# The ninth expert's first 1024 tokens in seven block products, and the next layers' units packed beside 24 steps instead of 40

## What is computed

```python
# L1: eight experts and one shared network, every token through all nine
g = jnp.einsum('bsd,edf->ebsf', h, Wg); u = jnp.einsum('bsd,edf->ebsf', h, Wu)   # D=256, F=1024
expert_outs = jnp.einsum('ebsf,efd->ebsd', jax.nn.silu(g) * u, Wd)
shared = jnp.einsum('bsf,fd->bsd', jax.nn.silu(h @ Sg) * (h @ Su), Sd)
x = x + (1.0 - sg) * jnp.einsum('be,ebsd->bsd', gating_probs, expert_outs) + sg * shared
# L2: adapter chosen per batch, residual, layer norm
h = jax.nn.relu(jnp.einsum('bsh,bha->bsa', x, w1) + b1)                          # A=64
y = x + jnp.einsum('bsa,bah->bsh', h, w2) + b2
x = x + layernorm(y) * gamma + beta
# L3: one 256x256 matrix chosen per batch
x = x + jnp.einsum('bnh,boh->bno', x, W) + b
```

## Time and profile before

| | us |
|---|---|
| median of 3 runs | 1586.52 (1586.15 to 1587.53) |
| the profiled execution, its own time | 1585.52 |
| its span, first to last instruction | 1583.7 |
| PE busy | 1574.8 (99%) |
| DVE, ACT, POOL busy | 1134.1, 931.1, 670.1 |

### The profile page before, as it was taken

The page is one execution under the profiler, slowest core; times in us unless marked ns, Lnnn a source line. Parts: engine busy times, 40 slices in busy tenths (PEclk is TensorE's granted clock), DMA queues, the critical chain, the costliest instruction groups (busy, mean ns, idle before and its releaser), DMA issues.

```text
span 1583.7 us, 22423 instructions
## 1 busy us (share of the span) xinstructions
PE 1574.8 (99%) x7916; PEld 1343.0 (85%) x7916; DVE 1134.1 (72%) x1685; ACT 931.1 (59%) x1683; POOL 670.1 (42%) x621
## 2 busy tenths in 40 slices
PE   9999999999999999999999999999999999999999
PEld 7888889999988888888888888888888888888898
DVE  6855556688789776776776776776776777657667
ACT  6655555565666666566656656666666665555444
POOL 7865544756777432442342342342342342028000
PEclk9999999999999999999999999999999999999999
DMA  4111105455421010010010010010010010022000
GB/s 161 55 53 53 54 27 188 159 174 173 162 92 40 14 41 27 14 41 27 14 40 27 14 41 27 14 40 28 14 41 28 14 40 27 14 58 78 14 14 28
DMA packets 31012, 85.98 MB, mean 54 GB/s; under 512 B 5030, under 2 KB 10534, under 8 KB 30774
## 3 DMA queue, kind: packets, MB, share of 16 engines
q1 hardware_dynamic: 30310, 83.21, 15.3%
q0 software_dynamic: 304, 1.10, 0.2%
q10 hardware_dynamic: 288, 0.26, 0.1%
HBM read 82.46 MB, written 2.10 MB: 53 GB/s over the span
## 4 chain that ended last, share of the span: by engine, by line
PE 94%; POOL 4%; issue 1%; DVE 1%; ACT 0%; DMA 0%; SPq 0%; POOLq 0%; ACTq 0%; DVEq 0%
PE up L674 13%; PE up L673 13%; PE up L672 13%; PE sum L441 12%; PE sum L443 12%; PE sum L442 12%; PE up L441 4%; PE up L442 3%; PE up L443 3%; PE up L449 2%; PE up L451 2%; PE up L450 2%; POOL expert_in L1479 1%; DMA raw<-in_shared 0%; POOL x_sums L1479 0%
## 5 line engine op out<-in xcount | busy, mean ns | idle before, releaser
L1291 ACT ACTIVATE hidden_hi<-up_tile 128x512 fp32r<-128x512 f32 x256 | 161.3, 630 | 188.5 <-DVE up_tile L2107 165.9
L2112 DVE TENSOR_TENSOR hidden_lo<-up_tile,hidden_hi 128x512 fp32r<-128x512 f32 x256 | 197.9, 793 | 44.7 <-ACT hidden_hi L1291 44.7
L2102 DVE TENSOR_TENSOR gate_tile<-up,gate_tile 128x512 f32<-128x512 f32 x192 | 130.1, 687 | 137.9 <-PE up L674 137.9
L441 PE MATMUL sum<-hidden_hi,down 128*128 128x512 f32 x512 | 199.3, 389 | 0.0
L672 PE MATMUL up<-x_sums,gate_up 128*128 128x512 f32 x512 | 199.2, 389 | 0.0
L443 PE MATMUL sum<-hidden_hi,down 128*128 128x512 f32 x512 | 199.2, 389 | 0.0
L673 PE MATMUL up<-x_sums,gate_up 128*128 128x512 f32 x512 | 199.2, 389 | 0.0
L442 PE MATMUL sum<-hidden_lo,down 128*128 128x512 f32 x512 | 199.2, 389 | 0.0
L674 PE MATMUL up<-x_sums,gate_up 128*128 128x512 f32 x512 | 199.2, 389 | 0.0
L2107 DVE TENSOR_TENSOR up_tile<-up_tile,gate_tile 128x512 f32<-128x512 f32 x192 | 183.5, 983 | 3.4 <-ACT gate_tile L1284 1.1
L1284 ACT ACTIVATE gate_tile<-gate_tile 128x512 f32<-128x512 f32 x192 | 119.7, 632 | 90.1 <-DVE gate_tile L2102 87.9
(11 more groups left out here) (332 smaller groups left out, 4014.6 us busy)
## 6 DMA issues: line engine op xcount, KB each, us to landing
raw<-in_experts SPq DMA_DIRECT2D x64, 512.0 KB, 3.2
raw<-in_l SPq DMA_DIRECT2D x51, 512.0 KB, 3.2
raw<-in_shared SPq DMA_DIRECT2D x23, 512.0 KB, 3.2
raw<-in_w SPq DMA_DIRECT2D x8, 256.0 KB, 2.5
x<-in_xT SPq DMA_DIRECT2D x3, 512.0 KB, 9.2
l_stage<-in_l SPq DMA_DIRECT2D x3, 512.0 KB, 4.1
out<-out_stage SPq DMA_DIRECT2D x6, 256.0 KB, 2.2
gate_w<-in_gw POOLq DMA_DIRECT2D x1, 1024.0 KB, 5.5
```

Of the source, the lines that this page charges most:

```text
L441: pe.matmul(out, wh, vh, start=start, stop=False)
L1291: A(hi[:, i], cu[:, i], ACT.Copy).then_inc(hi_done, 1)
L2102: V.tensor_tensor(t, ps, t, ALU.add).then_inc(c_done[m], 1)
L2112: V.tensor_tensor(lo[:, i], cu[:, i], hi[:, i].bitcast(f32), ALU.subtract).then_inc(lo_done, 1)
```

## The change

1. **Jobs.** The tokens 0 to 1023 of the ninth expert go as a seven-product block of their own: `PAIR_BLOCKS` has 17 entries, (8, 0) the last. `LAST_JOBS` keeps the jobs of 512, 256 and 256 tokens, 24 steps, whose weights are the blocks that the slots use (`gate_up`), with the one block that no slot needs in `plain_gate_up`.
2. **Units.** The five units stay (`UNITS`). Units 0 and 1 no longer follow a job each; their x is ready when the last slots are taken. `WHEN` places units 0 to 2 in steps 2 to 27 and unit 3 in 18 to 34; the last unit keeps its distance to the last step. Late weights are made at steps `LATE_AT` instead of one in each of steps 3 to 9.
3. **Places.** y, squares and the adapter's hidden tile get places of their own for unit 0, and two sets in `raw` for the others; the L3 matrices of batches 2 to 7 and the adapter matrices move to the weight sums' places; one pair of row sums instead of two. Some waits guard the new overlaps.
4. **Biases.** The L3 biases of batches 4 to 7 are loaded after the second adapter down product; `l2_up_stage(0)` waits for 12 bias loads: the eight of `b1` and four of L3.
5. **POOL's order.** The row sum and the power -1/2 of units 1 and 0 stand between late weights 5 and 7.

```diff
-LAST_JOBS = [(0, BLK), (BLK, BLK), (2 * BLK, BLK), (3 * BLK, S), (3 * BLK + S, S)]
+LAST_JOBS = [(2 * BLK, BLK), (3 * BLK, S), (3 * BLK + S, S)]
+UNITS = [(0, BLK), (BLK, BLK)] + LAST_JOBS
+LAST_STEPS = 8 * len(LAST_JOBS)
+ALL_STEPS = LAST_STEPS + 20
...
+PAIR_BLOCKS = [(e, j) for e in range(NS) for j in range(2)] + [(NS, 0)]
+NSS = len(PAIR_BLOCKS) * PAIRS
+LATE_AT = [1, 1, 3, 3, 4, 5, 6, 7]
...
-    (9, 10, 11, 11, 11, 11, 12, 12, 12, 13, 13, 13, 13, 14, 14, 14, 15, 15, 16, 16, 17, 18),
...
+    (2, 2, 4, 4, 4, 4, 5, 5, 5, 6, 6, 6, 6, 7, 7, 7, 8, 8, 10, 10, 11, 12),
+    (3, 6, 8, 9, 9, 9, 11, 11, 11, 12, 13, 12, 13, 15, 15, 15, 16, 16, 18, 18, 19, 19),
+    (10, 11, 13, 14, 14, 14, 17, 17, 17, 18, 19, 18, 19, 21, 21, 21, 22, 22, 24, 24, 26, 27),
+    (18, 18, 20, 21, 21, 21, 23, 23, 23, 24, 25, 25, 25, 26, 27, 27, 29, 29, 30, 32, 30, 34))]
...
-        def late_step(b):
-
-            return b + 3 if b < 6 else b + 2
...
         late_small = 2 * B
+        early_small = B + B // 2
...
                 sp.dma_start(b1[:, b:b + 1], b1_d[langs[b]]).then_inc(small_full, 16)
-                sp.dma_start(biasb[:, b], bias_d[subjs[b]].to_broadcast([P, D])).then_inc(small_full, 16)
-            for i in range(len(LAST_JOBS)):
+                if b < B // 2:
+                    sp.dma_start(biasb[:, b], bias_d[subjs[b]].to_broadcast([P, D])).then_inc(small_full, 16)
+            for i in range(len(UNITS)):
+                if i == 1:
+                    sp.wait_ge(l2_down, 2)
+                    for b in range(B // 2, B):
+                        sp.dma_start(biasb[:, b], bias_d[subjs[b]].to_broadcast([P, D])).then_inc(small_full, 16)
...
                 if i == 0:
-                    pe.wait_ge(small_full, 16 * late_small)
-                if i in (1, 2):
-                    pe.wait_ge(out_ready, 2 * i - 1)
+                    pe.wait_ge(small_full, 16 * early_small)
+                if i == 1:
+                    pe.wait_ge(gated_done, FT)
...
-            hooks.setdefault(9, []).insert(0, b2_stage)
+            hooks.setdefault(3, []).insert(0, b2_stage)
...
             for b in reversed(range(B)):
-                hooks.setdefault(late_step(b), []).insert(0, lambda b=b: late_hi(b))
+                hooks.setdefault(LATE_AT[b], []).insert(0, lambda b=b: late_hi(b))
...
             for b in range(B):
                 w3_plus_one(b)
+                if b == B - 1:
+                    row_sum_lo(1)
                 if b:
                     late_lo(b - 1)
+                if b == 6:
+                    row_sum(1)
+                    rstd_stage(0)
...
-            hooks.setdefault(9, []).append(center_b2)
+            hooks.setdefault(3, []).append(center_b2)
```

More of the change, by code:

```diff
@@ L155, in build @@
     ws = [place(f"weight_sums{s}", [P, 2, 7 * P], f32, over=f"gate_up{s}", skip=7 * K1) for s in range(PAIRS)]
-    xst = place("x_row_sum", [P, BLK], f32, over="raw", skip=14336)
-    xsr = [place(f"x_row_sum_parts{r}", [P, 2, BLK], f32r, over="weights", skip=(12 - 4 * r) * K1) for r in range(2)]
+    xst = place("x_row_sum", [P, BLK], f32, over="weights", skip=14 * K1)
+    xsr = place("x_row_sum_parts", [P, 2, BLK], f32r, over="weights", skip=12 * K1)
     cg = place("gate_tile", [P, 3, BLK], f32, over="weights", skip=88 * K1)
@@ L282, in last_steps @@
         def last_steps(step, hooks):
-            for T in range(40):
+            for T in range(LAST_STEPS):
                 job = T // FT
@@ L764, in last_up @@
                         b = (0, 1, 3, 2)[f % 2 * 2 + dt]
-                        c = slice(b * P, (b + 1) * P)
-                        last = product(ps, gul[f // 2][:, 0, m, c], gul[f // 2][:, 1, m, c],
+                        wt = [l21[f // 2][:, h, m] if b == 3 else gu[f // 2][:, h, m, b * P:(b + 1) * P] for h in range(2)]
+                        last = product(ps, wt[0], wt[1],
                                        xh[:, dt, tok:tok + N], xl[:, dt, tok:tok + N], dt == 0, dt == DT - 1)
@@ L985, in _ @@
             last_steps(last_step, hooks)
-            for T in range(40, 60):
-                if T < 42:
+            for T in range(LAST_STEPS, ALL_STEPS):
+                if T < LAST_STEPS + 2:
                     last_down(T - 2, S)
@@ L1348, in pair_tiles @@
                 tile_hi(k, 2)
[L1350 to L1353 removed]
+            for e, j in PAIR_BLOCKS:
+                for s in range(PAIRS):
+                    pair_tiles(e, j, s)
             tile_hi(NSS - 1, 3)
@@ L1732, in _ @@
                 mixed_lo_part(NB - 2, dt)
-            for e in range(NS):
+            for e in range(NE1):
                 weight_sums(e, 2)
@@ L1788, in late_lo @@
                 lo_part(w3[b][:, 1], raw[:, s, 0:512], w3[b][:, 0])
-                lo_part(w1r[:, b, 1], raw[:, s, 512:640], w1r[:, b, 0])
+                w1 = [gu[3][:, h, b // 4, 3 * P + b % 4 * P:4 * P + b % 4 * P] for h in range(2)]
+                lo_part(w1[1], raw[:, s, 512:640], w1[0])
                 lo_part(w2[b][:, 1], raw[:, s, 640:896], w2[b][:, 0]).then_inc(w_lo, 1)
@@ L2344, in out_stage @@
                 dve.wait_ge(l3_done, 2 * i + part + 1)
+                if i == 1 and not part:
+                    dve.wait_ge(mean_done, 3)
                 if i >= 2 and not part:
                     dve.wait_ge(stored[i % 2], 32 * (i // 2))
+                    dve.wait_ge(small_full, 16 * late_small)
                 V.tensor_tensor(ostage[:, i % 2, q:q + half],
```

248 lines of the change are left out of this document (122 added, 126 removed), and 3 rows, old and new, of the table WHEN.

## The result

| | before | changed |
|---|---|---|
| median of the runs | 1586.34 us (4 runs) | 1601.51 us (4 runs) |
| ratio | 1 | 1.0101, 95% [1.0089, 1.0114] |
| span of the profiled execution | 1583.7 us | 1599.4 us |
| granted clock of PE, mean | 1.00 | 0.995 |

The change makes the kernel slower, by 15.7 us in the profiled spans. The prediction had the direction and the first cause, and a time 6.5 us too low: 1601.5 lies above its range.

The account below looks back on a forecast made before the run. PE was taken as the bound, up to the last few microseconds. Products -5.4, wait for b1 +9.5 and dense stretch +4.5 sum to +8.6 us: span 1592.3, median forecast 1595.0 us, range 1588.5 to 1600.

Parts of the forecast that it names:

- Products: Sixteen steps of 512 tokens go (65.3 us), four seven-product slots come (59.8 us): 24 matmuls fewer, -5.4 us.
- The wait for b1: At unit 0's adapter product after step 4, PE waits for batch 7's b1 from about 1490.3 to 1499.9: +9.5 us.
- The bound of 10: Upper bound on PE's wait for b1, if the load's landing takes 2.9 us.
- its rival's working: If b1 came early, unit 0's mean product would still wait 3.3 us for centred b2; total 1588.9 us, chance 0.08.
- The clock: Rival: PE's clock falls to half in the b1 wait, costing 2.3 to 6.4 us, 1597.3 to 1601.4; chance 0.30.
- The dense stretch: Steps 8 to 23, 256 tokens each: PE and DVE equally loaded, six PE waits totalling 5.6 us, taken as +4.5.
- the diagonal after step 7: After step 7, PE waits 1.2 us for the diagonal.
- x_lo after 10: After step 10, PE waits 0.6 us for x_lo.
- the group in steps 22 to 25: In steps 22 to 25, PE waits 1.3 us.
- the squares after 13: After step 13, PE waits 1.2 us for the squares.
- those after 18 and 20: PE waits 0.6 us after step 18 and 0.7 us after step 20.
- From this 1.4 comes off: Unit 2's last L3 half moves behind the last down product, where PE has time: 1.4 us off the 5.6.

Follow-up runs that it names:

- e1: Changed kernel with the eight b1 loads issued with the cols loads, ahead of the late weights; 1592.03 us, ratio 1.005.
- e3: Changed kernel plus 44 matmuls of 512 columns, result overwritten, ahead of PE's wait for b1; 1597.71 us, ratio 1.0086.
- e11_after_tail: Changed kernel, behind the last down product: last take before unit 3's variance step, last unit's product before unit 2's second L3 half and unit 3's broadcast; 1601.27 us.
- e12: e1 with unit 2's second L3 half ahead of the last down product again, its output right behind the first half's; 1594.94 us, ratio 1.0062.
- e8: e1 with three DVE instructions of units 0 to 2 cut to 8 columns, so output is not the reference's; 1590.25 us, ratio 1.0027.
- e5: e1 with unit 3's stages from the down product to the broadcast one step earlier; 1597.81 us, ratio 1.0074.
- e7: e2 with unit 0's and unit 1's stages from the variance on one step later, and unit 3's table from e5; 1604.98 us, ratio 1.0119.
- e9: e1 with the order behind the last down product changed as in e11_after_tail; 1594.77 us, ratio 1.0064.
- e2: e1 with b2 centred first in DVE's list of step 3; 1590.60 us, ratio 1.0037.
- e1_again: e1 unchanged, run once more beside e12 on the same chip; 1594.27 us, ratio 1.0059.
- e4: e2 with three of the units' low-part splits of 512 tokens moved from DVE to POOL; 1591.82 us, ratio 1.0048.
- e10: e2 with the order behind the last down product changed as in e11_after_tail; 1592.86 us, ratio 1.0047.

## Why the prediction was wrong

It said 1595.0 with a range to 1600.0; the median was 1601.5. Step by step, in its own terms:

- **Products, -5.4: right.** -5.3 by the landmarks, good to some 2 us, and POOL, ACT and DVE kept up with the four added slots: PE has no wait before 1490.
- **The wait for b1, +9.5: right in mechanism, 1.2 too small.** 10.7. The chain fails at one link: "the split of unit 0's x, 1.29". It took 2.65 (below), so step 3's tile was gated at 1488.33 and not at 1487.0, and all behind it came as much later. The bound of 10 was too low for the same reason. Undone by e1, it was worth 6.7 to 8.1 us, clock included, and not 10.7, because the centred b2 was the next late supplier, at 4.7 where its rival's working said 3.3.
- **The clock, nothing in the sum: wrong.** I gave it 0.30 as a rival with 2.3 to 6.4 us. It fell, twice, for 2.9 in slow matmuls; filling the wait in e3 gave back 3.4. The median of 1601.5 fell on that rival's upper figure, 1601.4, by luck: the clock is less than half of its 6.4, and other terms make up the rest. The prediction's argument against was only that the trace of before has no row for it. The rule that it cited (the Trainium skill, TensorE: Matmul & The Clock Gate, "Why this matters for your kernels": an idle gap amid matmuls sends the clock to half) would have made it the forecast, and on the long wait the trace agrees, with 0.50 granted from 1496 on. The second fall, behind two waits of 0.9, came in this execution and not in e11_after_tail.
- **The dense stretch, +4.5: the waits near in sum, the tail wrong.** I had six waits of 5.6 together and the trace shows six before the last down product, of 4.6. Named and there: the diagonal after step 7 (0.6), x_lo after 10 (0.9), two of the group in steps 22 to 25 (0.4 and 0.6). Not named: unit 0's squares right behind the long wait (1.2) and DVE's take at 1532.7 (0.9). Named and absent are the squares after 13, which the second fall of the clock covers (1.3 in e11_after_tail, 1.5 in e1 and e3), and those after 18 and 20. So that 4.6 is near 5.6 is in part luck: 2.5 of what was named is absent, and 2.1 of what is there was not named. With 2.1 of short gaps the stretch cost 6.7. What failed is "From this 1.4 comes off, because unit 2's last L3 half ... now stands in the tail, where PE has time". PE has none to give there: between the last down product and the last unit's product it is busy with unit 3's variance product, the beta part, this half and the broadcast, and the tail, which the sum had at no change, is 2.9 longer. The variance product had moved into the tail too, and the prediction had no term for it. So the term measured 6.7 - 1.4 - 0.8 + 2.9 = 7.4. By e12's trace the half costs about as much on one side of the down product as on the other (1.3 and 1.5).
- **The sum:** +8.6 forecast, +15.7 measured: 1.2 of the wait, 2.9 of the clock, 2.9 of the term above, and 0.1 of the products make 7.1.

What stays open: e8 shows that less work on DVE is worth 3.6 to 5 us of e1's time, but not how much of that is load and how much shorter distances; each shift of a stage that was tried (e5 to e7, e9 to e11) ran into a neighbour. No version with seven products came level with the kernel before; the nearest correct one, e2, is 0.37% slower, and -5.3 us of products are in it.

## What to carry to other kernels

- A user that moves towards its supplier is to be costed by the whole list of things it waits for, in order of arrival: the first late one hides the next, so undoing it gives back only the distance between the two (10.7 and 4.7 here).
- When a stretch is moved to where "the engine has time", look at what is queued behind it on each of the engines that touch it. In a tail the chain hops between engines, and the view of waits shows next to nothing of it; compare landmark to end instead.
- Take a duration from a row with the same company on the other engines, not from the shortest row of that form (1.29 was taken for the split, 2.65 came).

## What the hardware showed that I had not expected

**DVE at half speed beside POOL.** The same four instructions of a unit's sum, at 1526 while POOL makes low parts and at 1576 while it is idle; ahead of the first the product with one operand in PSUM, also beside POOL. Timeline of DVE, then of POOL, of the changed kernel:

```profile
1483.86 2.65 DVE L2240 TENSOR_TENSOR x_lo<-x,x_hi 128x512 fp32r<-128x512 f32 x2
...
1525.26 1.28 DVE L2306 TENSOR_TENSOR y<-sum,y 128x512 f32<-128x512 f32 x2
1526.46 3.32 DVE L2316 SCALAR_TENSOR_TENSOR x<-x,l_cols,y 128x256 f32<-128x256 f32 x4
...
1576.29 1.66 DVE L2316 SCALAR_TENSOR_TENSOR x<-x,l_cols,y 128x256 f32<-128x256 f32 x4
```

```profile
1523.49 2.18 POOL L1486 TENSOR_TENSOR gate_up<-raw,gate_up 128x512 fp32r<-128x512 f32 x2
...
1526.32 1.90 POOL L1486 TENSOR_TENSOR gate_up<-raw,gate_up 128x512 fp32r<-128x512 f32 x2
1528.18 0.93 POOL L1486 TENSOR_TENSOR l_w<-raw,l_w 128x256 fp32r<-128x256 f32 x1
```

3.32 against 1.66 with both inputs in SBUF, 1.28 as ever with one in PSUM; and the split of unit 0's x 2.65 against 1.29. The Trainium skill says it in SBUF — State Buffer, "Who interferes with whom": a VectorE instruction with two SBUF inputs contends with a GpSimd instruction that reads SBUF, through a read interface that the two share, and the sharing is an exclusive lock. These rows agree. The trace of before had such a row too, the split of the same unit 0 beside POOL's low parts, and I had taken the 1.29 of a quiet stretch (timeline of DVE, before):

```profile
1456.38 2.54 DVE L2231 TENSOR_TENSOR x_lo<-x,x_hi 128x512 fp32r<-128x512 f32 x2 [0.73 <-ACT x_hi L1387]
```

No run here changed POOL's company alone, so for this kernel it is read from rows and not shown by an experiment.

**The clock falls after short waits too, but not each time.** At 1535, after two waits of 0.9 in steps of 256 tokens, the granted clock went to 0.50 for some three microseconds (the windows above). Four other traces, e1_again, e5, e11 and e12, have the same two waits, and the clock stays at 1.00 behind them. A wait of 2.5 brought it down in e2. The wait of 1.3 to 1.5 for unit 1's squares came with a fall in e2 and e9, and with none in e1, e1_again, e3, e4, e5, e10, e11 and e12. What decides between them is open. In all traces that have it, the wait of 4.7 brought a fall, but of different length: in e1 the clock was back at 1499, in its repetition at 1501, and that makes 1.3 of the 2.6 us between their spans. Such a wait adds spread to a kernel as well as time.
